# One maximum over two neighbouring banks for two over one each, with narrow products in a new order

## The chip, the cores and the metric

The kernel runs on one core of a Trainium2 chip. The metric is the device time of one execution in microseconds: 1561.24 us before, the median of two runs (1559.94 and 1562.54).

## The reference

Four sequences of 1024 tokens of 256 features pass through one block of three sub-layers and then a second, small attention; everything is fp32.

```
x = attention(ln(x), ln(x), Wq1, Wkv1, Wo1, bo1) + x          # 16 heads of 16 features, 1024 keys
x = attention(ln(x), context, Wq2, Wkv2, Wo2, bo2) + x        # the same heads, 154 context keys
x = geglu_ff(ln(x), Wff1, bff1, Wff2, bff2) + x               # 256 -> 2 x 1024 -> 256
sdpa:      probs = softmax(q @ k.T * 64 ** -0.5);  out = probs @ v
geglu_ff:  lin, gelu = split(h @ Wff1 + bff1);  h = lin * (gelu * sigmoid(1.702 * gelu));  h @ Wff2 + bff2
then:      one attention of the result over the context with 256 features and weights of its own, added to it
```

The softmax of the first attention needs, for each head and each of the 4 x 1024 queries, the largest of 1024 scores. That maximum is what the change is about.

## The kernel before

**Tiles.** The tokens are cut into 16 chunks of 256 queries. For the first attention a chunk has four units, each of four heads (`G`), so there are 64 units. A unit first finds the maxima: for each of 8 pairs of a head and 128 queries (`PAIRS`), PE multiplies the 128 queries with the 1024 keys in two products of 512 columns (`max_scores`, letter M), one into each of the two PSUM banks `ps_max0` and `ps_max1`, and DVE takes the maximum of each over its 512 columns (`max_half`, same letter) into `mxh`. When all 16 are there, DVE combines the two halves of all pairs in one small reduction into `mxq` (`max_pairs`, Q); PE turns the 128 x 8 maxima into 8 rows (`max_turn`, T), DVE negates them and splits them into two bf16 parts, and two DMAs put them beside the queries as two further rows, so that the products of the scores come out with the maximum taken off. In the first four units the 16 products go through all pairs with the first 512 keys and then with the second; the other units do the same before the change.

Then come the scores (`scores`, S): for each of 8 blocks of 128 keys two pairs of products of 256 columns, each pair into one of the banks `ps_s0` and `ps_s1`. ScalarE (ACT) takes the exponential of a bank into `probs`, and `values` (V) multiplies four heads' probabilities with their values, narrowly: four products side by side, each on 32 of the 128 columns of PE's array, into `ps_o`.

**Whole and narrow.** A product with 128 output rows can be issued as one that uses all columns of the array, or as four of 32 columns each (`tile_position`), which PE runs side by side. The variable `array` remembers which form the last product had. `columns()` is called by the value products, which have only 17 output rows a head. `whole()` is called by all products that are written in one form, the projections, the feed-forward products, the transpositions and the cross maxima. `score` follows whichever form is current: with four narrow products on L1438, with a whole one on L1441.

**The other work.** Beside attention four chains run: `pre` (p: layer norm and projections of a later chunk), `mid` (m: output projection of the first attention, layer norm, the cross queries), `cross` (c: maxima, scores and values of the attention to the context; its maxima are products of 154 columns, three to a group, on L1630) and `last` (l: output projection, feed-forward, the last attention). They lag attention by some chunks, so at first there is little beside attention, and at the end only chains.

**What sets the order.** `ORDERS` is a table of strings, one for each step of the pipeline, each letter a piece of work. All engines walk the same string, and each does its own part of a letter in that order; semaphores do the rest. An engine never goes past a waiting instruction. The wait that matters here stands in `max_scores`:

```
pe.wait_ge(g_mx, unit * 2 * PAIRS + max(0, i - 1))
```

Product i of a unit waits until maximum i - 2 is done, the one that read the bank it writes into.

## Time and profile before

| what | us |
|---|---|
| median of two runs | 1561.24 |
| the profiled execution, as the others are timed | 1565.36 |
| its span, first to last instruction | 1563.5 |
| PE (matmul) busy | 1499.9 |
| DVE busy | 1107.8 |
| ACT busy | 946.5 |
| POOL busy | 253.7 |

The span is 1.9 us shorter than the time of the same execution, and that execution is 4.1 us above the median. "Busy" of PE counts a product from its start to its modelled end, and since the next product starts before the last one ends, the distance between starts says better what one costs.

### The profile page before, as it was taken

How to read it: one execution, taken by the hardware profiler on the slowest of the kernel's cores; microseconds unless marked ns; L12 is line 12 of the kernel's file. 1: busy time of each engine (PE TensorE's matmuls, PEld its weight loads, DVE VectorE, ACT ScalarE, POOL GpSimd, SP SyncE). 2: the span in 40 equal slices, each digit the busy share in tenths (PEclk: the TensorE clock that was granted, in tenths of full speed). 3: DMA queues.
4: the chain of work that ended last, by engine and by line, in shares of the span. 5: the costliest groups of instructions: out<-in, count | busy, mean ns of one | idle time of the engine just before them, and what ended most of it. 6: DMA issues, size and time to landing. Idle time of an engine off the chain costs nothing.

```text
span 1563.5 us, 44474 instructions
## 1 busy us (share of the span) xinstructions
PE 1499.9 (96%) x18122; PEld 1012.7 (65%) x18122; DVE 1107.8 (71%) x2269; ACT 946.5 (61%) x1928; POOL 253.7 (16%) x347
## 2 busy tenths in 40 slices
PE   6899999999999999999999999999999999998897
PEld 5555545675766767576766757666666757675676
DVE  4477787868678686767768586877778696863543
ACT  4366777656656575575666566665656566674343
POOL 2210322111202111121211212101101010002110
PEclk9899999999999999999999999999999999999999
DMA  8823453465242342527333262435423151413210
GB/s 225 198 72 110 137 104 90 103 126 116 66 99 67 94 91 70 117 62 151 77 92 76 75 122 68 105 72 106 98 61 90 27 120 49 99 51 88 59 36 14
DMA packets 228865, 143.93 MB, mean 92 GB/s; under 512 B 92787, under 2 KB 220597, under 8 KB 228405
## 3 DMA queue, kind: packets, MB, share of 16 engines
q1 hardware_dynamic: 228597, 141.07, 38.5%
q8 instruction: 143, 2.34, 0.7%
q14 instruction: 61, 0.50, 0.1%
q10 hardware_dynamic: 64, 0.02, 0.0%
HBM read 92.68 MB, written 47.74 MB: 90 GB/s over the span
## 4 chain that ended last, share of the span: by engine, by line
PE 78%; DVE 10%; DMA 4%; SPq 3%; ACT 2%; issue 2%; POOL 0%; DVEq 0%; POOLq 0%; ACTq 0%
PE ps_o L1806 12%; PE ps_last L1714 11%; PE ps_last L1725 7%; PE ps_max L1438 6%; PE ps_s L1438 6%; PE ps_max L1441 5%; PE ps_s L1441 5%; PE ps_pre L1551 4%; PE ps_pre L1560 4%; DVE mxh L1398 3%; DMA den<-o_s 2%; PE ps_cross L1652 2%; PE ps_cross L1656 2%; PE ps_last L1560 2%; PE ps_last L1756 1%
## 5 line engine op out<-in xcount | busy, mean ns | idle before, releaser
L1398 DVE TENSOR_REDUCE mxh<-ps_max 128x1 f32<-128x512 f32 x1024 | 657.8, 683 | 109.9 <-PE ps_max L1441 72.1
L1181 ACT ACTIVATE probs<-ps_s 128x512 f32<-128x512 f32 x1024 | 572.9, 598 | 221.4 <-PE ps_s L1441 112.0
L1806 PE MATMUL ps_o<-probs,vg 128*17 128x256 f32 x4096 | 295.8, 382 | 0.2 <-ACT o_sb L1187 0.2
L1438 PE MATMUL ps_max<-kst,qst 96*32 96x512 bf16 x2156 | 198.6, 384 | 3.1 <-DVE mxh L1398 0.8
L1438 PE MATMUL ps_s<-qst,kst 98*32 98x256 bf16 x4448 | 198.5, 274 | 1.8 <-issue 1.5
L1441 PE MATMUL ps_max<-kst,qst 96*128 96x512 bf16 x485 | 159.3, 382 | 10.2 <-DVE mxh L1398 6.5
L1438 PEld LDWEIGHTS ps_s<-qst,kst 98*32 98x32 bf16 x4448 | 116.6, 96 | 78.8 <-ACT probs L1181 15.0
L1356 DVE SCALAR_TENSOR_TENSOR th<-th,gb 128x256 f32<-128x256 f32 x128 | 58.8, 459 | 151.6 <-ACT gb L1156 151.3
L1441 PE MATMUL ps_s<-qst,kst 98*128 98x256 bf16 x936 | 158.3, 273 | 1.1 <-ACT probs L1181 0.4
L1806 PEld LDWEIGHTS ps_o<-probs,vg 128*17 128x17 f32 x4096 | 99.7, 97 | 79.0 <-issue 32.4
L1714 PE MATMUL ps_last<-y_hi,wff_hi 128*128 128x256 f32 x448 | 139.7, 312 | 5.5 <-DVE hT L1359 3.6
L1714 PE MATMUL ps_last<-y_lo,wff_hi 128*128 128x256 f32 x448 | 126.3, 282 | 0.0
L1714 PE MATMUL ps_last<-y_hi,wff_lo 128*128 128x256 f32 x448 | 126.0, 281 | 0.0
L1725 PE MATMUL ps_last<-wff,hT 128*128 128x256 f32 x480 | 115.4, 387 | 0.4 <-DVE hT L1359 0.4
L1154 ACT ACTIVATE th<-ps_last,b_tanh 128x256 f32<-128x256 f32 x112 | 53.0, 474 | 96.8 <-PE ps_last L1714 96.5
L1132 ACT ACTIVATE probs<-ps_cross 128x512 f32<-128x512 f32 x140 | 84.5, 603 | 44.1 <-PE ps_cross L1441 37.0
L1441 PEld LDWEIGHTS ps_s<-qst,kst 98*128 98x128 bf16 x936 | 82.2, 98 | 40.7 <-ACT probs L1181 10.1
L1438 PEld LDWEIGHTS ps_max<-kst,qst 96*32 96x32 bf16 x2156 | 57.9, 95 | 71.9 <-DVE mxh L1398 48.2
L1725 PEld LDWEIGHTS ps_last<-wff,hT 128*128 128x128 f32 x480 | 90.5, 193 | 16.8 <-DVE hT L1359 1.7
L1714 PEld LDWEIGHTS ps_last<-y_hi,wff_hi 128*128 128x128 f32 x448 | 84.8, 189 | 25.6 <-DVE hT L1359 16.0
L914 POOL TENSOR_TENSOR qk_f<-qk_f,qk_parts 128x512 f32<-128x512 f32 x40 | 46.4, 1159 | 302.5 <-ACT qk_f L1107 158.3
L1714 PEld LDWEIGHTS ps_last<-y_lo,wff_hi 128*128 128x128 f32 x448 | 85.3, 190 | 0.6
(278 smaller groups left out, 2110.2 us busy)
## 6 DMA issues: line engine op xcount, KB each, us to landing
vg<-v_s SPq DMA_DIRECT2D x64, 272.0 KB, 3.6
parts_s<-qk_parts SPq DMA_DIRECT2D x28, 384.0 KB, 4.3
o_s<-o_sb SPq DMA_DIRECT2D x64, 128.0 KB, 2.0
o_s<-o_sb SPq DMA_DIRECT2D x32, 256.0 KB, 2.5
oT<-o_s SPq DMA_DIRECT2D x62, 128.0 KB
den<-o_s SPq DMA_DIRECT2D x62, 128.0 KB
q_s<-qk_parts SPq DMA_DIRECT2D x16, 384.0 KB, 2.5
q2st<-q_s SPq DMA_DIRECT2D x16, 384.0 KB, 5.5
```

Of the source, the lines that this page charges most:

```text
L1132: nc.scalar.activation(tile, cross_banks[spare][x % 2][:, :], ACT.Exp, scale=SCALE).then_inc(c_e, 1)
L1154: nc.scalar.activation(th[:, m % 2, :], bank[:, CH:2 * CH], ACT.Tanh, scale=GELU_A / 2, bias=b_tanh[:, m:m + 1]).then_inc(c_th, 1)
L1181: nc.scalar.activation(probs[:, step % PR, 2 * pair:2 * pair + 2, :].rearrange("p j q -> p (j q)"), ps_s[pair][:, :], ACT.Exp, scale=SCALE ...
L1356: nc.vector.scalar_tensor_tensor(th[:, m % 2, :], th[:, m % 2, :], 1.0, gb[:, m % 2, :], ALU.add, ALU.mult).then_inc(c_gt, 1)
L1398: nc.vector.tensor_reduce(mxh[:, i % PAIRS, i // PAIRS:i // PAIRS + 1], ps_max[i % 2][:, :], AX_X, ALU.max).then_inc(g_mx, 1)
L1438: last = mm(bank[j * W:(j + 1) * W, cols_], keys[:, j * W:(j + 1) * W], queries, start=True, stop=True, tile_position=(0, j * W))
L1441: last = mm(bank[:, cols_], keys, queries, start=True, stop=True)
L1551: last = mm(bank[:, m * CH:(m + 1) * CH], w[:, k, m * P:(m + 1) * P], y[:, k, :], start=(k == 0), stop=(k == KD - 1))
L1560: last = mm(bank[:, i * D:(i + 1) * D], y[:, k, i * P:(i + 1) * P], w[:, k, :], start=(k == 0), stop=(k == KD - 1))
L1714: last = mm(last_banks(o)[m % 2][:, part * CH:(part + 1) * CH], wff1[w][:, k, cols_], y3[y][:, k, :], start=(i == 0), stop=(i == len(terms ...
L1725: last = mm(bank_[:, i * D:(i + 1) * D], hTs[e][:, m, i * P:(i + 1) * P], wff2[:, m, :], start=(m == 0), stop=(m == FM - 1))
L1806: last = mm(ps_o[j * W:j * W + VW, 0:CH], vg[:, unit % VSLOTS, kt, j * VW:(j + 1) * VW], probs[:, step % PR, j, :], start=(kt == 0), stop= ...
```

## The change

From the fifth unit on (`unit >= HG`) the products are ordered pair by pair: product 2j takes the first 512 keys of pair j, product 2j + 1 the second, and both banks are one tensor of 1024 columns. One DVE instruction takes the maximum over all of them, straight into `mxq`, which now has two halves that alternate by unit; the combining reduction is gone for these units. Both products of a pair wait for the maximum of the pair before (`maxima_before(unit) + pair`). The first four units stay as they were.

The projections, the output and feed-forward products into 256 columns, the products of the last attention and the cross maxima no longer call `whole()`; a function `product` issues them in the form that is current, as `score` did. The short transpositions of the maxima become an ordinary narrow product with the identity where the form is narrow (`few_turned`). The long transpositions and the first feed-forward products stay whole. `ORDERS` is a new table.

```diff
--- before.py
+++ after.py
@@ -69,55 +69,56 @@
 ORDERS = (
...
-    "VQOTmSSVMSSMMSVMSMSpMSMSMSMSMSMVMusSMVMSMVMSSQVVpSTmSVMOpSmSVMoSMSVMSSMpMSSMMpMMSSMMpMMSSsVMMQpT"
...
+    "VSMMSSVSMuMVVSMMsMpMsMMsSMMSSSMMSSSopMMsTsMMSSVSOVMMuSVVSsMMSuVVMMSSMMSSQVSMMoSSSpMMSVSQSMMVVVTS"
...
@@ -227,7 +228,7 @@
         probs = sb("probs", [P, PR, G, CH])
         o_sb = sb("o_sb", [P, 2, CH])
         mxh = sb("mxh", [P, PAIRS, 2])
-        mxq = sb("mxq", [P, PAIRS])
+        mxq = sb("mxq", [P, 2, PAIRS])
         sh_hi = sb("sh_hi", [PAIRS, P], BF16)
         sh_lo = sb("sh_lo", [PAIRS, P], BF16)
 
@@ -324,7 +325,8 @@
             return part[:, k, cols_], ff1_raw[k][:, cols_]
 
 
-        ps_max = [ps(f"ps_max{i}", [P, 512]) for i in range(2)]
+        ps_both = ps("ps_max", [P, 1024])
+        ps_max = [ps_both[:, i * 512:(i + 1) * 512] for i in range(2)]
         ps_s = [ps(f"ps_s{i}", [P, 512]) for i in range(2)]
         ps_o = ps("ps_o", [P, 512])
         ps_last = ps("ps_last", [P, 512])
@@ -495,6 +497,10 @@
                     next(chains[letter])
             assert all(next(chain, None) is None for chain in chains.values())
 
+        def maxima_before(unit):
+
+            return min(unit, HG) * 2 * PAIRS + max(0, unit - HG) * PAIRS
+
         def wait_parts(engine, count):
 
             for p in range(min(count, MAX_LAG)):
@@ -1394,13 +1400,24 @@
 
             def max_half(k):
                 unit, i = divmod(k, 2 * PAIRS)
+                if unit >= HG:
+                    if i == 1:
+                        dve.wait_ge(g_mT, unit - 1)
+                    if i % 2:
+                        dve.wait_ge(g_mt, k + 1)
+                        nc.vector.tensor_reduce(mxq[:, unit % 2, i // 2:i // 2 + 1], ps_both[:, :], AX_X,
+                                                ALU.max).then_inc(g_mx, 1)
+                    return
                 dve.wait_ge(g_mt, k + 1)
                 nc.vector.tensor_reduce(mxh[:, i % PAIRS, i // PAIRS:i // PAIRS + 1], ps_max[i % 2][:, :], AX_X,
                                         ALU.max).then_inc(g_mx, 1)
 
             def max_pairs(unit):
-                dve.wait_ge(g_mx, (unit + 1) * 2 * PAIRS)
-                nc.vector.tensor_reduce(mxq[:, :], mxh[:, :, :], AX_X, ALU.max).then_inc(g_mp, 1)
+                if unit < HG:
+                    dve.wait_ge(g_mx, (unit + 1) * 2 * PAIRS)
+                    if unit > 1:
+                        dve.wait_ge(g_mT, unit - 1)
+                    nc.vector.tensor_reduce(mxq[:, unit % 2, :], mxh[:, :, :], AX_X, ALU.max).then_inc(g_mp, 1)
 
             def max_turned(unit):
                 dve.wait_ge(g_mT, unit + 1)
@@ -1431,15 +1448,25 @@
 
                 array["columns"] = True
 
-            def score(bank, cols_, keys, queries):
+            def product(bank, cols_, weights, moving, start, stop):
 
                 if array["columns"]:
                     for j in range(G):
-                        last = mm(bank[j * W:(j + 1) * W, cols_], keys[:, j * W:(j + 1) * W], queries,
-                                  start=True, stop=True, tile_position=(0, j * W))
+                        last = mm(bank[j * W:(j + 1) * W, cols_], weights[:, j * W:(j + 1) * W], moving,
+                                  start=start, stop=stop, tile_position=(0, j * W))
                 else:
-                    last = mm(bank[:, cols_], keys, queries, start=True, stop=True)
+                    last = mm(bank[:, cols_], weights, moving, start=start, stop=stop)
                 return last
+
+            def score(bank, cols_, keys, queries):
+
+                return product(bank, cols_, keys, queries, True, True)
+
+            def few_turned(bank, rows, x):
+
+                if array["columns"]:
+                    return mm(bank[0:rows, 0:P], x, ident[:, :], start=True, stop=True, tile_position=(0, 0))
+                return nc.tensor.transpose(bank[0:rows, 0:P], x, ident[:, :])
 
             def head():
                 def head_turn(p):
@@ -1545,20 +1572,18 @@
 
             def project(bank, w, y):
 
-                whole()
                 for m in range(KD):
                     for k in range(KD):
-                        last = mm(bank[:, m * CH:(m + 1) * CH], w[:, k, m * P:(m + 1) * P], y[:, k, :],
-                                  start=(k == 0), stop=(k == KD - 1))
+                        last = product(bank, slice(m * CH, (m + 1) * CH), w[:, k, m * P:(m + 1) * P], y[:, k, :],
+                                       k == 0, k == KD - 1)
                 return last
 
             def project_rows(bank, y, w):
 
-                whole()
                 for i in range(TT):
                     for k in range(KD):
-                        last = mm(bank[:, i * D:(i + 1) * D], y[:, k, i * P:(i + 1) * P], w[:, k, :],
-                                  start=(k == 0), stop=(k == KD - 1))
+                        last = product(bank, slice(i * D, (i + 1) * D), y[:, k, i * P:(i + 1) * P], w[:, k, :],
+                                       k == 0, k == KD - 1)
                 return last
 
             def stack_at(h):
@@ -1625,16 +1650,13 @@
                         else:
                             pe.wait_ge(c_mx, o * 2 * Q2F + f - 1)
                         i, h0, nh = q2_heads(f)
-                        whole()
                         for j in range(nh):
-                            last = mm(cross_max_banks[spare][f % 2][:, j * CTX:(j + 1) * CTX], q2st[0:ROWS, h0 + j, i * P:(i + 1) * P],
-                                      k2st[0:ROWS, h0 + j, 0:CTX], start=True, stop=True)
+                            last = score(cross_max_banks[spare][f % 2], slice(j * CTX, (j + 1) * CTX),
+                                         q2st[0:ROWS, h0 + j, i * P:(i + 1) * P], k2st[0:ROWS, h0 + j, 0:CTX])
                         last.then_inc(c_mt, 1)
                         yield
                     pe.wait_ge(c_mx, (o + 1) * 2 * Q2F)
-                    whole()
-                    nc.tensor.transpose(ps_cross[0:H * TT, 0:P], mx2[:, :, :].rearrange("p h i -> p (h i)"),
-                                        ident[:, :]).then_inc(c_mT, 1)
+                    few_turned(ps_cross, H * TT, mx2[:, :, :].rearrange("p h i -> p (h i)")).then_inc(c_mT, 1)
                     for _ in range(3):
                         yield
                     x, after = 0, 0
...
@@ -1772,14 +1791,16 @@
                     pe.wait_ge(g_slo, unit)
                 if i == PAIRS and c == 0:
                     pe.wait_ge(h_far[g // 2], 8 * 16)
-                pe.wait_ge(g_mx, unit * 2 * PAIRS + max(0, i - 1))
+                pe.wait_ge(g_mx, maxima_before(unit) + (pair if c else max(0, i - 1)))
                 score(ps_max[i % 2], slice(0, 512), qst[0:ROWS, h, q * P:(q + 1) * P],
                       kst[0:ROWS, h, half * 512:(half + 1) * 512]).then_inc(g_mt, 1)
 
             def max_turn(unit):
-                pe.wait_ge(g_mp, unit + 1)
-                whole()
-                nc.tensor.transpose(ps_max[0][0:PAIRS, 0:P], mxq[:, :], ident[:, :]).then_inc(g_mT, 1)
+                if unit < HG:
+                    pe.wait_ge(g_mp, unit + 1)
+                else:
+                    pe.wait_ge(g_mx, maxima_before(unit + 1))
+                few_turned(ps_max[0], PAIRS, mxq[:, unit % 2, :]).then_inc(g_mT, 1)
 
             def scores(k):
                 step, pair = divmod(k, 2)
```

The hunks left out at the end give four more products of `last` the same replacement of `whole()` and `mm` by `product`.

PE, the products of the sixth unit's maxima (`ps_max`) among the scores (`ps_s`) and values (`ps_o`), before:

```order
L1438 MATMUL ps_max<-kst,qst 32x512 x4
L1438 MATMUL ps_s<-qst,kst 32x256 x16
L1438 MATMUL ps_max<-kst,qst 32x512 x4
L1806 MATMUL ps_o<-probs,vg 17x256 x4
L1438 MATMUL ps_max<-kst,qst 32x512 x4
L1438 MATMUL ps_s<-qst,kst 32x256 x8
L1438 MATMUL ps_max<-kst,qst 32x512 x4
L1806 MATMUL ps_o<-probs,vg 17x256 x4
L1438 MATMUL ps_max<-kst,qst 32x512 x4
L1438 MATMUL ps_s<-qst,kst 32x256 x16
L1438 MATMUL ps_max<-kst,qst 32x512 x4
L1806 MATMUL ps_o<-probs,vg 17x256 x4
```

and now:

```order
L1455 MATMUL ps_s<-qst,kst 32x256 x8
L1827 MATMUL ps_o<-probs,vg 17x256 x8
L1455 MATMUL ps_max<-kst,qst 32x512 x8
L1455 MATMUL ps_s<-qst,kst 32x256 x16
L1455 MATMUL ps_max<-kst,qst 32x512 x8
L1455 MATMUL ps_s<-qst,kst 32x256 x16
L1827 MATMUL ps_o<-probs,vg 17x256 x4
L1455 MATMUL ps_s<-qst,kst 32x256 x8
L1455 MATMUL ps_max<-kst,qst 32x512 x8
L1455 MATMUL ps_s<-qst,kst 32x256 x24
L1455 MATMUL ps_max<-kst,qst 32x512 x8
L1455 MATMUL ps_s<-qst,kst 32x256 x8
```

Single products into alternating banks, each with a score or a value product between, have become pairs (x8 is two products of four narrow ones), which stand at each end of runs of scores.

DVE, the maxima of two later units (`mxh` and `mxq` from `ps_max`, then the negated maxima `sh_hi` and `sh_lo`), before:

```order
L1398 TENSOR_REDUCE mxh<-ps_max 128x1 x4
L1403 TENSOR_REDUCE mxq<-mxh 128x8
L1391 TENSOR_SCALAR sh_hi<-ps_max 8x128
L1393 SCALAR_TENSOR_TENSOR sh_lo<-ps_max,sh_hi 8x128
L1398 TENSOR_REDUCE mxh<-ps_max 128x1 x16
L1403 TENSOR_REDUCE mxq<-mxh 128x8
L1282 RECIPROCAL den_c<-den_c 128x32
L1391 TENSOR_SCALAR sh_hi<-ps_max 8x128
```

and now:

```order
L1397 TENSOR_SCALAR sh_hi<-ps_max 8x128
L1399 SCALAR_TENSOR_TENSOR sh_lo<-ps_max,sh_hi 8x128
L1408 TENSOR_REDUCE mxq<-ps_max 128x1 x8
L1397 TENSOR_SCALAR sh_hi<-ps_max 8x128
L1399 SCALAR_TENSOR_TENSOR sh_lo<-ps_max,sh_hi 8x128
L1408 TENSOR_REDUCE mxq<-ps_max 128x1 x2
L1288 RECIPROCAL den_c<-den_c 128x32
```

The sixteen half maxima and the combining reduction of a unit have become eight.

PE, the first cross maxima (`ps_cross` and `ps_pre` from `k2st`, `q2st`) of a chunk after 22 units, before:

```order
L1438 MATMUL ps_s<-qst,kst 32x256 x8
L1630 MATMUL ps_cross<-k2st,q2st 128x154 x3
L1630 MATMUL ps_pre<-k2st,q2st 128x154 x3
L1441 MATMUL ps_s<-qst,kst 128x256 x4
L1441 MATMUL ps_max<-kst,qst 128x512 x2
L1441 MATMUL ps_s<-qst,kst 128x256 x2
L1630 MATMUL ps_cross<-k2st,q2st 128x154 x3
L1806 MATMUL ps_o<-probs,vg 17x256 x4
L1438 MATMUL ps_s<-qst,kst 32x256 x16
```

and now:

```order
L1455 MATMUL ps_s<-qst,kst 32x256 x8
L1455 MATMUL ps_cross<-k2st,q2st 32x154 x12
L1455 MATMUL ps_pre<-k2st,q2st 32x154 x12
L1455 MATMUL ps_s<-qst,kst 32x256 x8
L1455 MATMUL ps_max<-kst,qst 32x512 x8
L1455 MATMUL ps_s<-qst,kst 32x256 x8
L1827 MATMUL ps_o<-probs,vg 17x256 x4
L1455 MATMUL ps_cross<-k2st,q2st 32x154 x12
L1827 MATMUL ps_o<-probs,vg 17x256 x4
```

Before, the cross maxima turned the form to whole, and scores and maxima after them were whole until the next value product; now all of the row stays narrow.

## Rows read from the trace of the kernel before

**Rows 1.** The page, busy us of each engine, share of the span, instructions.
```profile
PE 1499.9 (96%) x18122; PEld 1012.7 (65%) x18122; DVE 1107.8 (71%) x2269; ACT 946.5 (61%) x1928; POOL 253.7 (16%) x347
```

**Rows 2.** Waits: who <- for whom: us in total, times, longest.
```profile
PEld ps_max L1438 <- DVE mxh L1398: 48.2, 174, 0.7
...
PEld ps_max L1441 <- DVE mxh L1398: 19.4, 43, 3.0
...
PEld ps_last L1714 <- DVE hT L1359: 16.0, 40, 1.3
...
PEld ps_s L1438 <- ACT probs L1181: 15.0, 59, 0.5
```

**Rows 3.** Three stretches: length, busy us of PE, PEld, DVE, ACT, POOL; clock, DMA.
```profile
62.70:261.00 198.30, 191.12 (x2684) 106.93 (x2683) 154.13 (x292) 125.42 (x241) 41.21 (x47) 0.97 0.41 108
611.00:968.00 357.00, 352.55 (x4250) 242.54 (x4251) 267.99 (x554) 226.96 (x464) 64.69 (x84) 1.00 0.38 87
1325.90:1563.50 237.60, 212.88 (x2165) 155.47 (x2163) 123.64 (x276) 115.42 (x250) 28.13 (x41) 0.97 0.23 57
```

**Rows 4.** Timeline of PE in the middle: start, length, line, operands, shapes, count.
```profile
700.58 0.39 PE L1441 MATMUL ps_s<-qst,kst 98*128 98x256 bf16 x2
700.90 0.63 PE L1652 MATMUL ps_cross<-probs,v2b 128*17 128x256 f32 x8
701.34 0.61 PE L1656 MATMUL ps_cross<-probs,v2a 128*17 128x256 f32 x8
...
702.65 0.40 PE L1675 MATMUL ps_cross<-q2st,k2st 98*32 98x256 bf16 x8
702.87 0.40 PE L1438 MATMUL ps_max<-kst,qst 96*32 96x512 bf16 x4
703.09 0.40 PE L1438 MATMUL ps_s<-qst,kst 98*32 98x256 bf16 x8
703.42 1.99 PE L1725 MATMUL ps_last<-wff,hT 128*128 128x256 f32 x8
705.25 0.59 PE L1560 MATMUL ps_pre<-wo,oT 128*128 128x256 f32 x2
```

**Rows 5.** Timeline of PE from 388 us; idle before a row in brackets.
```profile
388.17 0.41 PE L1438 MATMUL ps_s<-qst,kst 98*32 98x256 bf16 x8
388.50 0.27 PE L1782 MATMUL ps_max<-ident,mxq 128*8 128x128 f32 x1
388.61 0.39 PE L1441 MATMUL ps_s<-qst,kst 98*128 98x256 bf16 x2
389.27 0.39 PE L1441 MATMUL ps_s<-qst,kst 98*128 98x256 bf16 x2 [0.28 <-ACT probs L1181]
389.50 0.36 PE L1630 MATMUL ps_cross<-k2st,q2st 96*128 96x154 bf16 x3
389.70 0.36 PE L1630 MATMUL ps_pre<-k2st,q2st 96*128 96x154 bf16 x3
```

**Rows 6.** Groups of PE, shapes apart: count, busy us, mean ns, idle before.
```profile
L1438 PE MATMUL ps_max<-kst,qst 96*32 96x512 bf16 x2156 | 198.6, 384 | 3.1 <-DVE mxh L1398 0.8
```

**Rows 7.** Groups of DVE, shapes apart: count, busy us, mean ns, idle before.
```profile
L1398 DVE TENSOR_REDUCE mxh<-ps_max 128x1 f32<-128x512 f32 x1024 | 657.8, 683 | 109.9 <-PE ps_max L1441 72.1 <-PE ps_max L1438 33.5
...
L1403 DVE TENSOR_REDUCE mxq<-mxh 128x8 f32<-128x16 f32 x64 | 10.6, 166 | 1.8
...
L1324 DVE TENSOR_REDUCE mx<-ps_pre 128x1 f32<-128x154 f32 x28 | 8.5, 302 | 0.0
```

**Rows 8.** Timeline of PE where only products of the maxima stand, from 62.9 us.
```profile
62.92 0.60 PE L1441 MATMUL ps_max<-kst,qst 96*128 96x512 bf16 x2
64.09 0.39 PE L1441 MATMUL ps_max<-kst,qst 96*128 96x512 bf16 x1 [0.57 <-DVE mxh L1398]
```

**Rows 9.** Timeline of DVE at the same place.
```profile
63.34 1.29 DVE L1398 TENSOR_REDUCE mxh<-ps_max 128x1 f32<-128x512 f32 x2 [1.91 <-PE ps_max L1441]
```

**Rows 10.** Timeline of ACT at the place of rows 5.
```profile
388.62 2.30 ACT L1181 ACTIVATE probs<-ps_s 128x512 f32<-128x512 f32 x4 [0.26 <-PE ps_s L1438]
```

More of the change, by code:

```diff
@@ new lines @@
+    "lSVSiVMMVcfScVMMQSVuScSMMoSVVSMMlSSVcSOmMMScSVSMMlVVccSSMMllSSMMVSSVVSSTlccSMMSlVmccVOSSMMlcSmSV"
+    "QMMcSlSSccVMMSlSVoVMMSSlVcScMMSSVVScSMMlcSSuOVMMcolcSTcVVcmmMMSmlSScVMMmlSSMuMQcmcMmMlMMScVSSMMl"
+    "MMlMMlTcMlMVcSlMMxcSSMMlVuMMSlSVdMMlVSSMMllOi",
+    "SMcMofSSVlMMSSlVSTVcSMMVcSSMMSSecVSMMSSVcMQMSccSVSMMoulVcOSSVMMSlMMSSlVVumoSMMSSVScSVTlSSccSMMlS"
+    "SQVVMMcclSVcMMSSOlSSMMVcScVVSSQMMlmSSVcMMlVmSSMMcSlMMcSSVclVSOScSVmmTlmVSScMMlSmcMMlMMQlocMMlMMl"
+    "MMclSSVcMMQumMMcVVSSTcmMMlScSMQMuScMMlxSMMSSVSMMVdolSlSMMSVOVMMlMMl",
@@ new lines @@
+    "SSSSTVQSMMVViSSMcMclSSVMMSScVVMMSuSVcSMMSScVSOMMSSeVcfScoMMSVVllSScMMllTSSVSclScVVSMMcuSlcOSSVVM"
+    "MclVVSScMMlmSVMMSQSlMSMccommVSVSVcSSMMlMcSSVMclMMSSOcVSlcSuTcSVScmmMMlScSVMMSVVSSMmMcSmScMMlmMMl"
+    "MMolMcMlMMlTclMMlcSmSMMlVMMScxMMSSlVVMudeMSloMMSSVSOMMlSMMlSQVV",
+    "STVSccSMiMSSVSMMcVSSlVMMScVSSMMSVScSOMMSccVSSMMlSlVcVMMfSlSSluVMMoScSVSVTSSlccmMSMSlcVocSSOVMMSl"
+    "cSVSVMMScSmlVMSMVmcSSlMcVMSSclMcMSSVVclVSScoMOSScmmlMScVmSSclSSQcVMMQmlmVTcSlcSlcSmVVlcSxSllSclS"
+    "SVlSldVSOVSleiVSSlSSVVSSVSVSVOVlQV",
@@ L1721, in last @@
                         pe.wait_ge(c_h, (o + 1) * FM - late * (1 - q))
-                    whole()
                     i = q // 2
                     for m in range((q % 2) * FM // 2, (q % 2 + 1) * FM // 2):
-                        last = mm(bank_[:, i * D:(i + 1) * D], hTs[e][:, m, i * P:(i + 1) * P], wff2[:, m, :],
-                                  start=(m == 0), stop=(m == FM - 1))
+                        last = product(bank_, slice(i * D, (i + 1) * D), hTs[e][:, m, i * P:(i + 1) * P], wff2[:, m, :],
+                                       m == 0, m == FM - 1)
                     if q == 3:
@@ L1735, in last @@
                 pe.wait_ge(c_tab, (o // CPB + 1) * 48)
-                whole()
                 for i in range(TT):
                     for k in range(KD):
-                        last = mm(bank_[:, i * CH:i * CH + CTX], den2s[e][:, k, i * P:(i + 1) * P], m3[:, k, :],
-                                  start=(k == 0), stop=(k == KD - 1))
+                        last = product(bank_, slice(i * CH, i * CH + CTX), den2s[e][:, k, i * P:(i + 1) * P], m3[:, k, :],
+                                       k == 0, k == KD - 1)
                 last.then_inc(c_s3, 1)
@@ L1752, in last @@
                 pe.wait_ge(c_pTc, o + 1)
-                whole()
                 for i in range(TT):
                     for a in range(2):
-                        last = mm(bank_[:, i * D:(i + 1) * D], p3Ts[late][:, a, i * P:(i + 1) * P], vp[:, a, :],
-                                  start=(a == 0), stop=(a == 1))
+                        last = product(bank_, slice(i * D, (i + 1) * D), p3Ts[late][:, a, i * P:(i + 1) * P], vp[:, a, :],
+                                       a == 0, a == 1)
                 last.then_inc(c_av3, 1)
@@ L1764, in max_scores @@
                 c, g = divmod(unit, HG)
-                pair, half = i % PAIRS, i // PAIRS
+                pair, half = (i // 2, i % 2) if c else (i % PAIRS, i // PAIRS)
                 h, q = g * G + pair // TT, pair % TT
```

86 lines of the change are left out of this document (37 added, 49 removed).

## The prediction

> **What bounds the kernel now.** I read the page's totals first. TensorE (PE) is busy for 1499.9 of the span's 1563.5 us, VectorE (DVE) for 1107.8, 71% [rows 1]. So the time is PE's own work plus the few places where PE waits, and work taken from DVE is worth nothing unless PE was waiting for it. The list of waits says how much that is: PE's weight loads wait 48.2 and 19.4 us for the row maxima, 15.0 us for the exponentials and 16.0 us for the hidden layer [rows 2]. The table by stretches shows where there is slack: from 62.7 to 261 us PE is busy 191.12 of 198.3 us, in a middle stretch 352.55 of 357.0, at the end 212.88 of 237.6 [rows 3]. The middle has little to give; the beginning has some, because there are few other jobs beside attention; the end has no attention left and the change reaches it only through its new order.
>
> **The change, part 1: PE's work.** The timeline gives the price of a product as the distance from its start to the next start. Inside narrow products, 8 of 256 columns (two groups of four) take 702.87 - 702.65 = 0.22 us; two whole ones of the same size take 389.50 - 389.27 = 0.23 us, so a group of four narrow products costs what one whole product costs, 0.11 us. A narrow pair that is followed by a whole product takes 703.42 - 703.09 = 0.33 us, a whole pair followed by narrow ones 700.90 - 700.58 = 0.32 us [rows 4, 5]. A change of form thus costs 0.11 and 0.10 us. In the program's order a transposition counts as whole whatever its shape: the one at 388.50 came 0.33 us after a narrow pair and gave way to a whole product after 0.11 us [rows 5]. Counted so, PE changes form 221 times each way before and 144 times now: 77 x 0.21 = 16 us less.
>
> Against this stand three prices. (a) 454 of the 512 products of 154 columns for the cross maxima become groups of four narrow ones. Three whole ones take 389.70 - 389.50 = 0.20 us, 0.07 each [rows 5]. No narrow group of that width is in the trace; by the columns it would be 154/256 x 0.11 = 0.07, and no more than the 0.11 of the wider group: 0 to 18 us more. I take 0 to 2, since four narrow products start together: the four maxima products from 702.87 on last 0.40 us where one alone has a mean of 384 ns [rows 4, 6], so their starts lie within some 0.02 us. The Trainium skill (TensorEngine Tiling (Array Packing), Instruction Overhead) speaks against it: each matmul carries about 60 cycles, so a short free dimension gains nothing. By that a narrow group would last about 0.10 us, an estimate, and the sum 14 us more; the row of the four starts does not bear it out. (b) 392 fp32 products of 256 columns and 32 of 154 become narrow too. The nearest row is the cross value product, 0.44 us for a group of four in two passes [rows 4], against 705.25 - 703.42 = 1.83 us for four whole ones, of which 0.10 is their change of form: 0.43 each. Even; I put 0, with 4 us (0.01 x 424) as the other end. (c) 50 short transpositions become two-pass products of 128 columns, half of 0.44 instead of 0.11 us [rows 4, 5]: 50 x 0.11 = 5 us more. PE's work: -16 + 5 + 2 = **-9 us**, between -11 and +11.
>
> **Part 2: DVE.** 480 reductions over 1024 columns replace 960 over 512, and 60 small ones go. A reduction lasts 302 ns over 154 columns and 683 over 512 [rows 7], 1.064 ns a column, so 683 + 512 x 1.064 = 1.23 us for 1024. Drawn from the 16-column reduction of 166 ns instead, the slope is 1.042 and the result 1.22; two of the old ones, 1.37, are the upper end. I take 1.22. That frees 480 x (2 x 0.683 - 1.22) + 60 x 0.166 = 80 us of an engine that is not the bound: 0 on the path by itself.
>
> **Part 3: the hand-over, which is what counts.** Before, two banks took turns: product n waits for maximum n-2, so product n-1 lies under the wait. Now both banks are read by one instruction, and the first product of a pair waits for the whole maximum of the pair before. One link is readable where nothing else stands: product at 62.92, its maximum at 63.34 (0.42 later), 0.683 long, next product in that bank at 64.09 (0.06 to 0.07 after its end) [rows 7, 8, 9]. From a product's start to the next in its bank is therefore 0.42 + 0.68 + 0.06 = 1.16 us at least before, and now, from the second product of a pair to the first of the next, 0.42 + 1.22 + 0.06 = **1.70 us**. Less the product's own 0.22, 1.48 us of other PE work must stand between two pairs, or PE waits for the rest. PE is in order, so the scores and values queued behind that product wait with it, and ScalarE behind them.
>
> I priced the order with the prices above, leaving out the first four units, which keep the old form. Before, 89 of 840 places are shorter than 1.16 us, by 16 us in all. Now 176 of the 480 pairs are shorter than 1.70, by 49 us: 27 of them in units 4 to 15 (the first 260 us), 22 in the other 48. The first excerpt of the order shows why: "ps_max x8, ps_s x16, ps_max x8" leaves 0.44 us where 1.48 are wanted.
>
> The scores have the same kind of link: the second half of a score pair starts 0.11 after 388.17, at 388.28, its exponential at 388.62, each lasting some 0.58 (2.30 for four), and the next pair in that bank starts at 389.27 [rows 5, 10], about 0.97 us. Shorter than that are 50 of 960 places before, by 9 us, and 122 now, by 29 us, because the new order groups three or four scores.
>
> Where one wait falls within the window of another it is paid once. Going through the order so, the two together come to 18 us before and 55 now (with the turn of the maxima, which now waits for a 1.22 us reduction); simply added, 25 and 78. In the trace the starts at these places are further apart than the prices by 25 us at products and 10 at scores (less than the weight loads wait [rows 2], since those run ahead of the products); that lies above the counted sums, so the method does not overstate. The waits grow by 36 us (paid once) to 53 (added). I take **+36**, and **-5**, a third of the 16.0 us for the hidden layer [rows 2], for other waits that shrink when PE comes later.
>
> **Sum**: -9 + 36 - 5 = +22 us on the profiled execution's 1565.4, 1587. That execution is 4 us above the median of 1561.2, so in the measure of the runs 1561.2 + 22 = **1583 us**, 1.4% more. Within 2% (about what a measurement of this kernel can tell from no change) is 1530 to 1592.
>
> **Rivals.**
> 1. *The hand-over is paid in full.* If the windows don't cover each other, waits grow by 53, PE's work falls by 9: 1605 us, slower. With the cross groups at 0.11 us, 1621. It decides once the waits grow by more than 40 us. For it: in the trace the waits before were 1.4 times the counted ones. Against: a PE that waits for a maximum lets exponentials catch up. Chance 0.29.
> 2. *Short narrow groups have a floor.* If four narrow products never take less than the 0.11 us that four of 256 columns take [rows 4], the 454 cross groups cost 18 us more than whole ones, 16 more than I took: 1599, slower by 2.4%. For it: no shorter group is in the trace. Against: the four starts within 0.02 us [rows 4, 6]. By the Trainium skill's 60 cycles (the page and section named above) it would be 1595, an estimate. Chance 0.08.
> 3. *The lighter DVE answers sooner.* DVE now has 60 instructions fewer between maxima, 80 us less work, and where today a maximum waits behind other DVE work the pair's wait is shorter than counted; the hidden layer's chain, which runs through DVE, gets shorter as well. Then the waits do not grow: -9 - 5 = 1547. To be faster by over 2% they would have to shrink by 22 us beside PE's 9, which is most of the 35 at products and scores. Against it, the middle stretch leaves only 5 us of idle PE in 357 [rows 3]. Chance 0.13, of which 0.09 below 1530.
>
> The forecast has 0.50. Of it a little lies beyond 1592, of rivals 1 and 2 a little within it: **faster 0.09, same 0.53, slower 0.38**. The range must leave out no more than 0.2: from 1543 (rival 3's ordinary case) to 1614 (rival 1 between its two prices).
>
> **What will show it.** In the profile after: reductions of 128x1024 at 1.2 us, x480; narrow cross products with starts 0.07 apart per group (0.10 would be rival 2); idle PE ahead of the products, put down to the maxima, most of all between 63 and 270 us, where the stretch that takes 198 us should take some 15 us longer; the middle about equal. DVE's busy time should fall to about 1030 us. PE's busy time tells less, since narrow products overlap in it. The forecast is wrong if the first 270 us are not longer, or if the reduction takes much other than 1.2 us.

## The result, and the profile after

The changed kernel takes 1615.78 us (median of two runs, 1615.07 to 1616.48) against 1561.24 before: 1.0354 times, 95% interval 1.0324 to 1.0384, 54.5 us longer. The prediction said 1583, at most 1614. All times below are medians; the kernel before, run again beside each group of experiments, gave 1560.5 to 1561.5.

The page's totals of the changed kernel:

```profile
PE 1520.8 (94%) x24439; PEld 986.5 (61%) x24439; DVE 1075.4 (67%) x1729; ACT 949.1 (59%) x1928; POOL 251.5 (16%) x347
```

PE has 6317 more products, since four narrow ones stand for one whole one, and a larger busy time than in [rows 1]. Busy time counts every product to its modelled end, so it says little here. The waits of the changed kernel say more (who <- for whom: us in total, times, longest):

```profile
PEld ps_max L1455 <- DVE mxq L1408: 70.5, 179, 1.9
...
PEld ps_s L1455 <- ACT probs L1187: 47.2, 130, 0.8
...
PEld ps_last L1736 <- DVE hT L1365: 20.6, 50, 1.3
...
PE ps_max L1455 <- DVE mxq L1408: 12.7, 28, 1.6
...
PEld ps_max L1458 <- DVE mxq L1408: 9.6, 25, 0.9
...
PEld ps_max L1458 <- DVE mxh L1412: 8.6, 16, 1.1
...
PEld ps_s L1458 <- ACT probs L1187: 3.6, 12, 0.8
```

In the kernel before, beside [rows 2]:

```profile
PEld ps_s L1441 <- ACT probs L1181: 10.1, 34, 0.6
...
PE ps_max L1441 <- DVE mxh L1398: 6.5, 15, 2.7
```

The waits for the maxima grew from 48.2 + 19.4 to 70.5 + 9.6 + 8.6 (the 8.6 in the first four units, which keep their form), and at the products themselves, after the weights were loaded, from 6.5 to 12.7 on the longest line. Those for the exponentials grew from 15.0 + 10.1 to 47.2 + 3.6 (narrow and whole scores; more scores are narrow now), and those for the hidden layer from 16.0 to 20.6 instead of shrinking.

Where along the span? The next two fences show the same stretches of work, cut at the starts of the 9th, 207th, 458th and 708th product for the maximum and at the last one; this is the table by stretches with the columns of [rows 3], of the kernel before and then of the changed one.

```profile
62.92:261.29 198.37, 191.19 (x2686) 107.15 (x2684) 154.42 (x292) 125.49 (x242) 40.99 (x47) 0.97 0.41 108
614.42:969.53 355.11, 350.66 (x4252) 240.85 (x4254) 266.60 (x551) 227.04 (x464) 64.69 (x84) 1.00 0.39 88
969.53:1397.94 428.41, 422.42 (x5365) 280.13 (x5361) 327.41 (x667) 270.10 (x554) 46.23 (x67) 1.00 0.37 83
```

```profile
60.68:280.33 219.65, 198.30 (x3328) 104.10 (x3327) 150.63 (x213) 127.97 (x246) 42.08 (x48) 0.96 0.38 101
639.48:996.85 357.37, 350.58 (x5958) 231.52 (x5954) 257.07 (x409) 226.59 (x460) 64.56 (x84) 1.00 0.38 89
996.85:1448.74 451.89, 436.89 (x7435) 280.44 (x7431) 318.81 (x495) 276.31 (x566) 46.48 (x67) 1.00 0.35 80
```

The first stretch is 21.3 us longer and the last 23.5; the middle one only 2.3 (the stretch ahead of it, whose ends can be read from the fences, 6.0). The losses stand where a unit of attention holds little else for PE. Counted from the starts in both traces, units 5, 6 and 9 (the first is 0) hold no other work of PE at all; from the first product of their maxima to that of the next unit they take 17.0, 16.8 and 16.8 us where they took 12.3, 12.2 and 11.9. In the 31 of the 60 changed units with less than 7 us of PE's other work the waits at maxima and scores grew from about 33 to 75 us, in the other 29 from about 6 to 16. One such place in the changed kernel, first PE, then DVE (timelines; start, length, line, operands, count, idle before in brackets):

```profile
222.73 0.62 PE L1455 MATMUL ps_max<-kst,qst 96*32 96x512 bf16 x8 [0.25 <-DVE mxq L1408]
223.17 0.61 PE L1455 MATMUL ps_s<-qst,kst 98*32 98x256 bf16 x16
223.61 0.61 PE L1827 MATMUL ps_o<-probs,vg 128*17 128x256 f32 x8
224.67 0.62 PE L1455 MATMUL ps_max<-kst,qst 96*32 96x512 bf16 x8 [0.46 <-DVE mxq L1408]
```

```profile
223.40 1.22 DVE L1408 TENSOR_REDUCE mxq<-ps_max 128x1 f32<-128x1024 f32 x1 [0.72 <-PE ps_max L1455]
```

The second product of the pair starts 0.22 after 222.73, at 222.95; its maximum starts 0.45 later and lasts 1.22; the next pair starts 0.05 after the maximum's end. The link is 224.67 - 222.95 = 1.72 us. Between the pairs stand two pairs of scores (16 narrow products, 0.44) and the values of one step (0.44), so PE waits 0.62 more than its work of 1.32 in a period of 1.94, and DVE itself is idle 0.72 in each.

For the whole trace I took each group's start-to-start distance less its price in the prediction's manner (prices of rows of the two traces) and counted what is above. **PE's priced work fell by 14.7 us (1418.0 to 1403.3), the waits rose by 67 (133 to 200)**: 34 at products for the maximum (31.9 to 66.1), 20 at scores (11.0 to 31.5), 12 elsewhere. 67 - 15 = 52, against the 51.1 us by which the profiled execution grew (1565.4 to 1616.5). These are sums over the starts of all products, and no single line of a view shows them.

### The profile page after: what moved, and what is told of

It is laid out like the page before. It is cut to its first block, busy times and chain, and to the rows that moved or that the text cites. A ratio compares the mean times of both kernels' runs of the same rounds, so it can differ in the third digit from the quotient of the medians.

```text
span 1614.7 us, 56629 instructions
## 1 busy us (share of the span) xinstructions
PE 1520.8 (94%) x24439; PEld 986.5 (61%) x24439; DVE 1075.4 (67%) x1729; ACT 949.1 (59%) x1928; POOL 251.5 (16%) x347
## 4 chain that ended last, share of the span: by engine, by line
PE 74%; DVE 12%; ACT 5%; issue 4%; DMA 3%; SPq 1%; POOL 1%; DVEq 0%; ACTq 0%; POOLq 0%
PE ps_last L1736 11%; PE ps_o L1827 10%; PE ps_max L1455 10%; PE ps_s L1455 8%; PE ps_last L1455 7%; DVE mxq L1408 5%; PE ps_pre L1455 4%; PE ps_pre L1458 3%; PE ps_last L1458 3%; PE ps_max L1458 3%; PE ps_s L1458 3%; PE ps_cross L1674 2%; ACT probs L1187 2%; PE ps_cross L1678 1%; PE ps_cross L1455 1%
## 5 line engine op out<-in xcount | busy, mean ns | idle before, releaser
L1408 DVE TENSOR_REDUCE mxq<-ps_max 128x1 f32<-128x1024 f32 x480 | 584.8, 1218 | 199.3 <-PE ps_max L1455 155.6
L1455 PE MATMUL ps_s<-qst,kst 98*32 98x256 bf16 x6456 | 295.4, 274 | 10.3 <-ACT probs L1187 5.6
L1455 PE MATMUL ps_max<-kst,qst 96*32 96x512 bf16 x3088 | 246.8, 383 | 19.6 <-DVE mxq L1408 12.7
L1455 PEld LDWEIGHTS ps_s<-qst,kst 98*32 98x32 bf16 x6456 | 165.5, 96 | 130.5 <-ACT probs L1187 47.2
L1455 PEld LDWEIGHTS ps_max<-kst,qst 96*32 96x32 bf16 x3088 | 68.1, 95 | 100.6 <-DVE mxq L1408 70.5
L1736 PEld LDWEIGHTS ps_last<-y_hi,wff_hi 128*128 128x128 f32 x448 | 84.8, 189 | 36.7 <-DVE hT L1365 20.6
L911 POOL TENSOR_SCALAR ve<-mv 128x2 f32<-128x2 f32 x34 | 7.7, 226 | 527.6 <-DVE mv L1268 527.6
L1458 PE MATMUL ps_max<-kst,qst 96*128 96x512 bf16 x252 | 81.5, 391 | 7.9 <-DVE mxh L1412 3.1
L1736 PEld LDWEIGHTS ps_last<-y_hi,wff_lo 128*128 128x128 f32 x448 | 85.1, 190 | 0.0
L1455 PE MATMUL ps_last<-wff,hT 128*32 128x256 f32 x1376 | 82.9, 379 | 0.0
L1458 PE MATMUL ps_s<-qst,kst 98*128 98x256 bf16 x434 | 74.3, 277 | 0.8 <-ACT probs L1187 0.7
```

The lines of the kernel that those rows point to most:

```text
L1408: nc.vector.tensor_reduce(mxq[:, unit % 2, i // 2:i // 2 + 1], ps_both[:, :], AX_X, ALU.max).then_inc(g_mx, 1)
L1455: last = mm(bank[j * W:(j + 1) * W, cols_], weights[:, j * W:(j + 1) * W], moving, start=start, stop=stop, tile_position=(0, j * W))
L1458: last = mm(bank[:, cols_], weights, moving, start=start, stop=stop)
L1736: last = mm(last_banks(o)[m % 2][:, part * CH:(part + 1) * CH], wff1[w][:, k, cols_], y3[y][:, k, :], start=(i == 0), stop=(i == len(terms ...
```

## The experiments

**1. One part at a time.** Three kernels: narrow products alone, with the old maxima and the old table; the new table with two maxima again, by turns and through the first keys of all pairs before the second, as before the change, and their combining at the end of a unit; one maximum in the old table.

```diff
 e1: ORDERS of the kernel before; maxima, combining and waits of before; product(), few_turned() of the change
 e2: ORDERS of the change; max_half as before, combine(unit) at the last product
 e3: ORDERS of the kernel before; everything else as changed
```

> The narrow products alone: two maxima over 512 columns and their combining, the waits and the order table of the kernel before, with the products that follow the current form and the short narrow transpositions. By the hand-over theory (the loss is PE waiting for the 1024-column maximum) this loses nothing and gains the changes of form: they fall from 221 each way to 149, PE's own work by 14 us, the waits stay: 1546 to 1552 us. By the rival that narrow products are dearer than they look (a floor, or more instructions on PE) it is 1575 us or more.

> The changed kernel with the maxima of the kernel before: two over 512 columns by turns in the two banks, the combining right after the last of a unit; new order and narrow products stay. Counted as in the prediction, products that come too early for their bank fall from 176 (54 us) to 30 (3 us); scores that do stay at 182 (32 us). Hand-over theory: 1561 to 1575 us, with PE's wait for the maxima nearly gone and that for the exponentials as in the changed kernel. Rival (the new order itself is the loss, whatever the maximum): 1600 us or more.

> The changed kernel with the order table of the kernel before: one maximum over 1024 columns, narrow products, old order. The old order puts other work between every two products, so a pair's second product comes late and the next pair's first soon after it: 266 of 480 pairs stand closer than 1.70 us, by 248 us. Hand-over theory: 1700 us or more, and the new order is then what keeps the one maximum bearable. Rival (the new order is the loss): below 1600 us.

Measured: e1 1569.13 us (ratio 1.0057, 1.0036 to 1.0077), e2 1623.34 (1.0402, 1.0377 to 1.0427), e3 1856.22 (1.1893, 1.1856 to 1.193). Waits of e1, then of e3:

```profile
PEld ps_max L1445 <- DVE mxh L1403: 60.2, 198, 2.7
PEld ps_s L1445 <- ACT probs L1186: 29.0, 102, 0.6
```

```profile
PEld ps_max L1454 <- DVE mxq L1407: 277.0, 237, 2.7
PEld ps_max L1457 <- DVE mxq L1407: 52.8, 49, 4.1
```

e1 missed my first theory and stayed below the second: PE's priced work fell by 13.8 us, and the waits grew by 17 (between the two profiled executions, which are 3.7 us apart; the medians are 8 apart), so 14 us less work ran longer. e3 came out as its first theory said: the one maximum needs a table laid out for it. e2 came out longer than the whole change, a surprise, and on the side of its rival. Part of that is the experiment's: the new table puts other letters between the two products of a pair, and DVE, in order, now stopped at the first one, and a product into `ps_pre` waited 15.3 us in 13 places (0.7 in the changed kernel) for the normalized output that DVE does behind it. Experiment 3 is the cleaner form.

**2. The length of the reduction.** The one maximum over 512 of the 1024 columns (the other half of the keys is left out of the shift), all else as changed.

```diff
-                        nc.vector.tensor_reduce(mxq[:, unit % 2, i // 2:i // 2 + 1], ps_both[:, :], AX_X,
+                        nc.vector.tensor_reduce(mxq[:, unit % 2, i // 2:i // 2 + 1], ps_both[:, 256:768], AX_X,
```

> The changed kernel, its maximum taken over the middle 512 of the 1024 columns only (half of the keys' scores are left out of it, so the shift of the exponentials is not the true maximum): same order, same waits, same instructions, only the reduction is 0.68 instead of 1.22 us. Hand-over theory: the time wanted between pairs falls from 1.70 to 1.17 us, the counted sum from 54 to 6 us: 1566 to 1580 us. Rival (the loss is the order of scores or a coupling of the two banks, not the length of the reduction): 1605 us or more.

Measured: 1589.61 us (1.0188, 1.0162 to 1.0214). The waits of this kernel:

```profile
PEld ps_s L1455 <- ACT probs L1187: 60.7, 161, 0.8
...
PEld ps_max L1455 <- DVE mxq L1408: 8.2, 17, 1.8
```

The wait listed for the maximum nearly vanishes (70.5 to 8.2), yet the time falls by 26 us only, between the two theories: the scores wait 13.5 us more. Start to start, PE's waits between the pairs of a unit fall from about 46 us to 6, and the kernel before has about 20 at the same products. So the long reduction holds 26 of the 54 us; 28 remain with a reduction of the old length, and they are not waits between the pairs.

**3. Two maxima at the place of the one.** e2 with that taken out: both reductions are issued at the second product.

```diff
+                elif i % 2:
+                    for half in range(2):
+                        dve.wait_ge(g_mt, k + half)
+                        nc.vector.tensor_reduce(mxh[:, i // 2, half:half + 1], ps_max[half][:, :], AX_X,
                                                 ALU.max).then_inc(g_mx, 1)
```

> The changed kernel with its new order, but two maxima over 512 columns, both issued where the one over 1024 stood, and their combining behind the last of a unit. A bank comes free after its own half, some 0.65 us earlier for the first of the next pair. Theory 1 (the longer hand-over and the new order each cost about half): 1585 to 1602 us, waits of PE before its products for the maximum about 25 us where the changed kernel has 66. Theory 2 (the longer hand-over is the whole loss): 1570 or less. Theory 3 (the new order is the whole loss): 1608 or more.

Measured: 1599.19 us (1.0244, 1.0222 to 1.0266). That is in the range of theory 1: in the new table two maxima are 16.6 us better than one. The waits before products for the maximum came to 33 us (expected about 25), before scores to 37.

**4. Is PE's work the time?** The first cross product of each of the 192 groups issued twice, in the kernel before (e6) and the changed one (e8), and the narrow products made whole again in the changed one (e7).

```diff
 e6, e8
-                        for j in range(nh):
+                        for j in [0, *range(nh)]:
 e7: whole() again ahead of the products that the change made narrow
```

> The kernel before, with the first product of every group of the cross maximum issued twice (192 more products of 67 ns, 12.9 us of PE's work; the output is the same). Theory 1 (around those products the length of a window is set by the maxima and exponentials, and PE's work fills it): 1561 to 1567 us, the added work taken out of waits. Theory 2 (PE's work adds up to the time): 1571 to 1577.

> The changed kernel, with the first product of every group of the cross maximum issued twice (12.9 us of PE's work more, as in the run on the kernel before; the output is the same). Theory 1 (more of the changed kernel's time is set by hand-overs than of the one before, so it takes up the added work): 1616 to 1621 us. Theory 2 (PE's work adds up): 1627 to 1632.

> The changed kernel with one maximum and the new order, but its newly narrow products made whole again (the form changes of the array come back, about 15 us of PE's work by the durations in the traces). Theory 1 (the narrow products' saving has come back as waits): 1612 to 1622 us. Theory 2 (the saving is in the time): 1627 to 1634.

Measured: e6 1570.22 (1.0054, 1.0035 to 1.0072), e8 1621.83 (1.039, 1.0369 to 1.0411), e7 1622.22 (1.0384, 1.036 to 1.0409). 12.9 us of work cost 9 in the kernel before, between the two theories, and 6 in the changed one; whole products, 26 us of priced work in the new table and not the 15 I had expected, cost 6. The intervals of e7 and e8 touch the changed kernel's, so 6 is not well known, but both are well under the work added and just past the end of their first theories' ranges. Neither kernel turns PE's work into time one for one, the changed one least. Read the other way, e7 says that in the new table the narrow products save some 6 us, where in the old one they lost 8 (e1).

**5. A failed test: easing the tables.** To free the tight places I moved letters of scores and products for the maximum by up to ten places, by the prices and links above: in the changed kernel (e9), in experiment 3 (e10), in e1 (e11).

```diff
 e9, e10, e11: ORDERS alone; the same letters in each string, S and M moved by at most ten places
```

> The changed kernel with one maximum; only its written-out order is eased: letters of scores and of products for the maximum are moved by at most ten places within a string, so that more of PE's other work lies between two scores of one bank and between a maximum and the next pair, by the durations in the traces. Theory 1 (two causes: places that the new order set too tight, and a hand-over of the long maximum that no order hides where a unit holds too little other work): 1600 to 1608 us, the tight scores' part only. Theory 2 (the order's tight places are not a cause): 1612 or more. Theory 3 (the order alone is at fault): 1590 or less.

> The kernel with the new order and two maxima in one place, its order eased in the same way for the shorter hand-over. Theory 1 (its loss of 38 us over the kernel before is tight places of the order, which two short maxima allow to be eased): 1568 to 1582 us. Theory 2 (tight places are not the cause): 1593 or more.

> Narrow products alone (two maxima, the order of the kernel before), with that order eased in the same way for the narrow products' shorter windows. Theory 1 (the narrow products' 14 us came back as waits at places that had just fitted, and easing them gives it back): 1552 to 1563 us. Theory 2 (the saving is lost elsewhere): 1567 or more.

Measured: 1708.92 (1.0947, 1.0902 to 1.0992), 1726.8 (1.1073, 1.1046 to 1.11) and 1660.5 (1.0641, 1.062 to 1.0662): 91 to 128 us longer than the kernels they came from. DVE's wait in e11, and then in e1:

```profile
DVE th L1361 <- ACT gb L1161: 192.5, 120, 4.7
```

```profile
DVE th L1361 <- ACT gb L1161: 154.2, 116, 4.7
```

A letter moves in every engine's queue. DVE stood 38 us longer ahead of the activation's second half, and the maxima queue behind it; PE's waits at products for the maximum rose from 41 to 81 us in e11. That the first is the cause of the second is my reading; no run isolates it. My reckoning held PE's order and two links only. These three runs say nothing on the tight places; they do say that a table moved by PE's prices alone can lose far more than it was to gain.

**6. The scores' link, with no table touched.** Exponentials over 256 of a bank's 512 columns (the other half is left out): in the changed kernel (e12), in the kernel before as control (e13), and in the changed kernel together with experiment 2 (e14).

```diff
-                nc.scalar.activation(probs[:, step % PR, 2 * pair:2 * pair + 2, :].rearrange("p j q -> p (j q)"),
-                                     ps_s[pair][:, :], ACT.Exp, scale=SCALE).then_inc(g_e, 1)
+                n = CH if step < PR else CH // 2
+                nc.scalar.activation(probs[:, step % PR, 2 * pair:2 * pair + 2, 0:n],
+                                     ps_s[pair][:, :].rearrange("p (j q) -> p j q", j=2)[:, :, 0:n],
+                                     ACT.Exp, scale=SCALE).then_inc(g_e, 1)
```

> The changed kernel with the self-attention's exponentials over 256 of a score bank's 512 columns (the other half is left out; the probabilities there are old values), so that a score bank comes free about 0.2 us earlier; order and maxima untouched. Theory 1 (places where scores follow each other too closely hold part of the loss): 1594 to 1605 us, waits before scores from 31 to under 18 us. Theory 2 (the time saved there comes back as waits before the next maximum): 1610 or more.

> Control: the kernel before with the same halved exponentials. Theory 1: its order leaves the scores more room (waits before scores 11 us), so it gains little: 1551 to 1558 us, at least 8 us less gain than the changed kernel. Theory 2: both gain the same, within 4 us.

> The changed kernel with the maximum over half the columns and the exponentials over half the columns, both left out as in the two runs that have one of them. Theory 1 (the two hand-overs hold most of the loss, side by side): 1560 to 1575 us. Theory 2 (the rest of the loss is elsewhere in the new order): 1582 or more.

Measured: e12 1611.73 (1.0331, 1.0312 to 1.0349), e13 1558.26 (0.9977, 0.996 to 0.9994), e14 1572.09 (1.0074, 1.0056 to 1.0093). Waits of e12, then of e14:

```profile
PEld ps_max L1457 <- DVE mxq L1410: 80.4, 182, 2.3
...
PEld ps_s L1457 <- ACT probs L1188: 16.6, 51, 0.6
```

```profile
PEld ps_s L1457 <- ACT probs L1188: 23.7, 73, 0.6
...
PEld ps_max L1457 <- DVE mxq L1410: 11.3, 19, 2.1
```

These runs say most. Shortening the scores' link alone gives 4 us, about what it gives the kernel before (3), so the second theories of e12 and e13 held: of the 19 us that PE no longer waits at scores (31.5 to 12.3 by start-to-start), 13.5 return at the maxima (66.1 to 79.6), since both links run side by side. Shortening the maximum alone gives 26. Both give 44, more than 4 + 26 and within e14's first theory. Once the maximum is short, the scores' link is worth 17.5 us in the new table (1589.6 to 1572.1), against 3 in the old one (e13), where both maxima are already over 512. At equal lengths of both links (512 for a maximum, 256 for an exponential) the changed kernel is 14 us above the kernel before (1572.1 and 1558.3), with full exponentials 28. Start to start, e14 waits about 6 us less than e13 at the maxima, but about 11 more at the scores, 9 more at the cross maxima and 6 more at the first feed-forward products.

**7. Narrow products with short links.** The kernel before (e15) and e1 (e16), both with maxima over 256 of 512 columns and exponentials over 256 of 512.

```diff
 e15, e16: the exponentials of experiment 6, and
-                nc.vector.tensor_reduce(mxh[:, i % PAIRS, i // PAIRS:i // PAIRS + 1], ps_max[i % 2][:, :], AX_X,
+                nc.vector.tensor_reduce(mxh[:, i % PAIRS, i // PAIRS:i // PAIRS + 1], ps_max[i % 2][:, 0:256], AX_X,
```

> The kernel before with every maximum over 256 of its 512 columns and the exponentials over 256 of 512 (the other halves are left out). Both hand-overs get some 0.2 us shorter. Theory 1 (half of the 43 us of waits before products for the maximum and scores are such hand-overs): 1535 to 1550 us. It is the base for the next run.

> Narrow products alone (two maxima, the order of the kernel before), with the same halves left out. Theory 1 (the saving of narrow products had gone into hand-overs; with these short it shows): 8 to 14 us less than the run before it. Theory 2 (the saving is lost elsewhere): no less, or up to 8 us more, as with full hand-overs.

Measured: e15 1539.83 (0.9863, 0.9844 to 0.9882), e16 1541.99 (0.9883, 0.9865 to 0.9901). The narrow products' loss of 8 us is 2 here, inside the intervals, and their 14 us do not show, as the second theory had it. Waits in e16 are 17 us above those in e15: 12 at maxima and scores, 5 at the cross maxima. The links may be part of it, but 8 and 2 are not clear of each other's noise; the rest stays open.

## Why the prediction was wrong

**PE's work, -9.** In the work it was -14.7. The form changes were right: 144 instead of 221 each way. Price (a) was right: groups of four narrow cross products start 0.07 apart, as here, where one stands between values and scores (timeline of the changed kernel's PE):

```profile
237.87 0.24 PE L1455 MATMUL ps_pre<-k2st,q2st 96*32 96x154 bf16 x4
237.94 0.77 PE L1455 MATMUL ps_s<-qst,kst 98*32 98x256 bf16 x16
```

That ends rival 2. By the Trainium skill (TensorEngine Tiling (Array Packing), Instruction Overhead) it would have been 0.10, an estimate; the trace does not agree. Price (b) was right, 0.43. Price (c) has two sides: a narrow short transposition delays the start of the next group by 0.01 us on average, but it holds its own columns for the 0.22 that I put (last section). The -14.7 goes by the starts of groups and hardly counts that; at 0.22 for all 50 transpositions up to 50 x 0.21 = 10 us of the saving would be gone, and the same in e1. How much of it is paid no run shows. **But the step from work to time failed too.** I took PE's saving as time because PE was busy 96% of the span. In the changed kernel 26 us of work (e7) and 12.9 (e8) are worth some 6 us each, in the kernel before 12.9 are worth 9 (e6), and in e1 14 us less work, by the starts, gave none. That the windows around the maxima, the exponentials and the turns have lengths of their own, which PE's work fills, fits these runs; window by window it is not shown.

**DVE.** The reduction lasts as I said:

```profile
L1408 DVE TENSOR_REDUCE mxq<-ps_max 128x1 f32<-128x1024 f32 x480 | 584.8, 1218 | 199.3 <-PE ps_max L1455 155.6 <-PE ps_max L1458 42.2
```

1218 ns, against 1.22. DVE's busy time fell to 1075, not 1030: I added mean lengths, but neighbouring reductions overlap (1024 of 683 ns showed 657.8 us busy, [rows 7]). Rival 3 is out: with the lighter DVE the waits grew.

**The hand-over, +36.** The mechanism, the link of 1.70 us (1.72) and its place in the first 260 us (predicted 15 us longer, 21 measured) were right. Sorted by what kept PE waiting, the links' own lengths grew by 26 us at the maxima (8.4 to 34.4) and 11 at the scores (2.9 to 13.8): 37, the number that "paid once" gave (its 55 - 18 is 37, put down as 36). Experiments 2 and 6 bear "paid once" out as a mechanism too, since either link covers the other's wait.

**What failed is what I left beside it.** I put -5 for "other waits that shrink when PE comes later". They grew: by 7 us at the first product of a unit (5.0 to 12.3), which waits for the turned maxima of the unit before; by 3 at scores whose exponential stood behind other work of ACT; by some 8 more at maxima and scores, at places that I could not sort; by 12 in all at the first feed-forward products (22.7 to 26.8), turns (16.8 to 20.8), transpositions, values and cross products. So this term was +30 where I had -5, without a row for it. With -9 + 36 - 5 = +22 against -15 + 67 = +52, waits came to 67 instead of 31, and 6 us more of PE's work went than I had: the 30 us missing. Some of the +30 will be PE's saved work come back as waits; e7 puts what came back at about 26 - 6 = 20 us in the changed kernel, wherever it stands, and that 6 is not well known. Rival 1 was nearest by number (1605) and by its mark (waits grow by over 40), but not by its mechanism: the windows do cover each other. (The range's lower end, 1543, was meant as rival 3's case, which its own sum puts at 1547; nothing here hangs on it.)

**Where the 54 us are**, by the experiments: 26 with the length of the one maximum (experiment 2); about 14 with scores that follow each other too closely once the maximum is not in the way (17.5 - 3, experiment 6); 14 left at equal links. In the other order the first two are 4 and 40, since the links cover each other. That the new table sets the scores too close is likely but not separated from the narrow products, as no run has the new table with short links and whole products. The third part is not resolved. The narrow products do not explain it plainly: they cost 8 in the old table with full links (e1) and 2 with short ones (e16), and in the new table they save some 6 (e7). Nor was a changed version found that beats the kernel before at full work.

The last stretch I did not foresee in its size. I counted 22 us of short places in the 48 later units and expected the middle to be about even; it was, but the last 428 us grew by 23.5, nearly as much as the beginning.

## What to carry to other kernels

Before joining two double-buffered banks into one instruction, take the time from the last product of the joined set to the first of the next (here 1.72 us against 1.16) and ask, stage by stage, whether other work of that length exists: eight pairs at 1.72 + 0.22 = 1.94 need 15.5 us in a unit, and the three units with no other work went from 12 to 17 us. An engine that is busy 96% of the time need not turn saved work into time where its in-order work sits between hand-overs; test it by taking that work away alone, since added work cost 9 of 12.9 us here (e6) while removed work gave nothing (e1). And when an order is laid out anew, a wait that did not hurt can grow, so a term for "other waits" should not be taken as a gain without a row for it.

## What the hardware showed that I had not expected

A two-pass narrow transposition holds only its own columns, and the others pass it, as the timeline of PE in the changed kernel shows:

```profile
316.97 0.61 PE L1455 MATMUL ps_s<-qst,kst 98*32 98x256 bf16 x16
317.41 0.27 PE L1468 MATMUL ps_max<-ident,mxq 128*8 128x128 f32 x1
317.41 0.30 PE L1455 MATMUL ps_pre<-k2st,q2st 96*32 96x154 bf16 x6
317.52 0.27 PE L1468 MATMUL ps_max<-ident,mxq 128*8 128x128 f32 x1
317.55 0.38 PE L1455 MATMUL ps_pre<-k2st,q2st 96*32 96x154 bf16 x5
317.70 0.40 PE L1827 MATMUL ps_o<-probs,vg 128*17 128x256 f32 x3
317.76 0.23 PE L1455 MATMUL ps_pre<-k2st,q2st 96*32 96x154 bf16 x1
317.83 0.38 PE L1827 MATMUL ps_o<-probs,vg 128*17 128x256 f32 x1
```

The transposition uses one of the four groups of columns. Products that come after it in the program, six of the next twelve, start from 317.41 on, ahead of its second pass at 317.52. Its own columns are behind by two passes: the last of the twelve starts at 317.76, 0.21 after the first of its group at 317.55, and the value product on these columns at 317.83, 0.13 after the other three. In 28 of the 33 places of this trace where at least seven narrow groups follow such a transposition, the slowest product of a group is soon about 0.22 us late and stays so until PE next waits, while the group's first one starts 0.01 to 0.12 late. So it is cheap where a wait follows that covers the 0.22; whether it costs time elsewhere no run here separates. The Trainium skill (TensorEngine Tiling (Array Packing), Key Properties) says that tiles operate independently; the trace agrees for products of different column groups.
